# Routed experts of an audio tower: weights stationary and 512 rows moving in the upper products

## What is computed

```python
scores = jax.nn.softmax((xf @ gate_w).astype(jnp.float32), axis=-1)
_, sel = jax.lax.top_k(scores + expert_bias[None, :], TOPK)      # TOPK = 2, E = 8
...
token_idx = order // TOPK
routed_in = xf[token_idx] * top_scores_sorted[:, None]           # rows of one expert together
h = jax.nn.silu(jax.lax.ragged_dot(routed_in, w1, counts)) * jax.lax.ragged_dot(routed_in, w3, counts)
routed_out = jax.lax.ragged_dot(h, w2, counts)                   # w1, w3: 512 x 448, w2: 448 x 512
out = out.at[token_idx].add(routed_out)
```

## Time and profile before

| | us |
|---|---|
| median of 3 runs (6222.33 to 6225.37) | 6224.54 |
| the profiled execution | 6225.23 |
| its span, first to last instruction | 6223.5 |
| TensorE busy | 6034.7 |
| VectorE busy | 3931.3 |
| ScalarE busy | 2617.3 |
| GpSimd busy | 2608.1 |

### The profile page before, as it was taken

How to read it: one execution, slowest core, us unless ns; L and a number is a source line. 1 busy time by engine, 2 the same in 40 slices (tenths; PEclk the granted TensorE clock), 3 DMA queues, 4 the chain that set the end, 5 groups by cost and what they waited for, 6 DMA issues and landing times. The chain is left out here.

```text
span 6223.5 us, 108360 instructions
## 1 busy us (share of the span) xinstructions
PE 6034.7 (97%) x32968; PEld 5134.6 (83%) x32968; DVE 3931.3 (63%) x9812; ACT 2617.3 (42%) x4904; POOL 2608.1 (42%) x1865
## 2 busy tenths in 40 slices
PE   5999999999999999999999996999999999999999
PEld 4888888888888888888888885888888888888888
DVE  4777777777777777777777774444444444444444
ACT  3444444444444444444444442333333333333332
POOL 1333333333333333333333333555555655555554
PEclk8999999999999999999999998999999999999999
DMA  2111111111111111111111113555555555555541
GB/s 69 48 44 44 47 41 47 44 44 47 42 49 41 46 45 43 48 41 48 43 44 47 42 40 102 138 143 141 143 144 143 132 140 145 137 143 144 143 105 48
DMA packets 273407, 495.61 MB, mean 80 GB/s; under 512 B 39444, under 2 KB 112148, under 8 KB 273236
## 3 DMA queue, kind: packets, MB, share of 16 engines
q1 hardware_dynamic: 202452, 363.37, 19.6%
q0 software_dynamic: 70912, 131.71, 10.4%
HBM read 370.13 MB, written 140.28 MB: 82 GB/s over the span
## 5 line engine op out<-in xcount | busy, mean ns | idle before, releaser
L1325 POOL DMA_INDIRECT out_dram<-res,goal x280 | 519.4, 1855 | 929.9 <-DVE res L1261 446.1
L619 ACT ACTIVATE e<-ps,shift 128x512 f32<-128x512 f32 x512 | 347.9, 684 | 671.1 <-DVE shift L718 635.3
L1193 ACT ACTIVATE rT_hi<-ps 128x512 fp32r<-128x512 f32 x280 | 167.9, 600 | 1040.2 <-PE ps L1129 1040.2
L1119 PE MATMUL ps<-e_hi,rT_hi 128*128 128x448 f32 x2240 | 596.9, 388 | 5.2 <-ACT rT_hi L1193 5.2
L1303 POOL TENSOR_TENSOR e_lo<-raw,e_hi 128x1792 fp32r<-128x1792 f32 x140 | 568.6, 4062 | 9.8 <-ACT e_hi L1188 6.5
L1261 DVE COPY res<-ps 128x512 f32<-128x512 f32 x280 | 193.7, 692 | 594.8 <-PE ps L1119 579.8
L1119 PE MATMUL ps<-e_lo,rT_hi 128*128 128x448 f32 x2240 | 550.8, 367 | 0.0
L1119 PE MATMUL ps<-e_hi,rT_lo 128*128 128x448 f32 x2240 | 549.4, 367 | 0.0
L904 POOL TENSOR_SCALAR ve<-ag 125x1 f32<-125x1 f32 x256 | 57.1, 223 | 1124.7 <-DVE ag L734 1087.0
L1119 PEld LDWEIGHTS ps<-e_hi,rT_lo 128*128 128x128 f32 x2240 | 421.2, 188 | 37.8
L1119 PEld LDWEIGHTS ps<-e_lo,rT_hi 128*128 128x128 f32 x2240 | 421.2, 188 | 37.3
(11 more groups left out here) (203 smaller groups left out, 15377.0 us busy)
## 6 DMA issues: line engine op xcount, KB each, us to landing
raw<-in_L_ffn_w SPq DMA_DIRECT2D x210, 896.0 KB, 5.6
X<-in_x SPq DMA_DIRECT2D x128, 750.0 KB
normed_rows<-y SPq DMA_DIRECT2D x128, 250.0 KB
out_dram<-h SPq DMA_DIRECT2D x128, 250.0 KB
rows<-normed_rows,entries POOLq DMA_INDIRECT x280, 4.8
out_dram<-res,goal POOLq DMA_INDIRECT x280
routed_entries<-entry,slot POOLq DMA_INDIRECT x256
raw<-in_L_ffn_sw SPq DMA_DIRECT2D x3, 896.0 KB
```

Of the source, the lines that this page charges most:

```text
L619: nc.scalar.activation(e[:, i, :], ps[:, (i + 1) % 2, :], ACT.Exp, scale=QS, bias=shift[:, i:i + 1], accum_out=total[:, i:i + 1]).then_inc ...
L1119: ins = nc.tensor.matmul(dst, lhs[a][:rows_, k, :], rhs[b][:rows_, k, 0:width], start=(k == 0 and i == 0), stop=(k == KC - 1 and i == 2))
L1325: nc.gpsimd.indirect_dma_start(out, bass.IndirectOffsetOnAxis(ap=goal[group[1] % 2][:, i:i + 1], axis=0), res[i % 2][:], None, bounds_chec ...
```

## The change

The upper products swap their roles. Stationary is now a block of 128 columns of a weight, moving are all 512 turned rows of the group, so the inner values come out with their columns on partitions and the four transposes per tile of `turn_hidden` go. The 448 columns are three full chunks of 128 and a tail of 64. w1 and w3 lie side by side in one tile (`W13`), w3 with its tail first, so that one block of 128 columns holds the tails of both; `up` (12 matmuls) runs 7 times a group. The lower product takes the inner values as they are: 3 full chunks in three passes, 9 matmuls, and a tail of 2 matmuls over 128 partitions, which hold the high part above and the low part below, against w2's tail stored twice: 11 matmuls a tile instead of 12.

With that, rows are scaled by their score on ScalarE (`scale_rows`, in place) before they are turned, and `half`, `half2` go; the turned rows of the whole group must be complete before its first product; turned rows and inner values have one buffer for a group instead of two for a tile. The gate of the tail needs w3's half, which sits on the upper 64 partitions, so ScalarE copies it to `evb` first. `inner_lo` and the last product of the tail's gate read two SBUF tiles. There are four result buffers instead of two, and `down` alternates between two PSUM banks. GpSimd's order is new: add 2, gathers 0 and 1, add 3, gathers 2 and 3, both splits, adds 0 and 1. w3 is fetched with two DMAs and w2 with three.

The core of the diff:

```diff
-            raws = (raw1, raw3, raw2)
-            W = [tuple((sbuf(f"e{n}_hi{p}", r.shape, F32R, c2), sbuf(f"e{n}_lo{p}", r.shape, F32R, c2))
+            W13 = [[sbuf(f"up_{part}{p}", [P, KC, 2 * HID], F32R, c2) for part in ("hi", "lo")] for p in range(2)]
+            W2 = [[sbuf(f"down_{part}{p}", [P, T, D], F32R, c2) for part in ("hi", "lo")] for p in range(2)]
+            rT = [sbuf(f"rT_{part}", [P, KC, GROUP], F32R, c2) for part in ("hi", "lo")]
+            uT = [sbuf("uT_hi", [P, T, GROUP], F32R, c2), sbuf("uT_lo", [P, FULL, GROUP], F32R, c2)]
+            res = [sbuf(f"res{i}", [P, D], F32, c2) for i in range(T)]
...
+                        sp.dma_start(raws[1][:, :, 0:TAIL], third[:, :, FULL * P:HID]).then_inc(w_in[1].of(group), 16)
+                        sp.dma_start(raws[1][:, :, TAIL:HID], third[:, :, 0:FULL * P]).then_inc(w_in[1].of(group), 16)
...
+                    def up(group, bank, col):
+
+                        w = W13[group[1] % 2]
+                        for i, (a, b) in enumerate(PASSES):
+                            for k in range(KC):
+                                ins = nc.tensor.matmul(ps[:, bank, :], w[a][:, k, col:col + P], rT[b][:, k, :],
+                                                       start=(k == 0 and i == 0), stop=(k == KC - 1 and i == 2))
+                        return ins
...
+                        if i == 0:
                             pe.wait_ge(w_lo[2].sem, w_lo[2].at(group))
+                            pe.wait_ge(uT_lo.sem, uT_lo.at(tile_of(group, FULL - 1)))
+                        pe.wait_ge(res_sb.sem, res_sb.at(back(t, 2)))
+                        for n, (a, b) in enumerate(PASSES):
+                            for k in range(FULL):
+                                nc.tensor.matmul(ps[:, 6 + i % 2, :], uT[a][:, k, i * P:(i + 1) * P], w[b][:, k, :],
+                                                 start=(k == 0 and n == 0), stop=False)
+
+                    def down_tail(group, i):
+
+                        w = W2[group[1] % 2]
+                        if i == 0:
+                            pe.wait_ge(uT_lo.sem, uT_lo.at(tile_of(group, FULL)))
...
+                        pe.wait_ge(w_lo[0].sem, w_lo[0].at(group))
+                        pe.wait_ge(w_lo[1].sem, w_lo[1].at(group))
+                        pe.wait_ge(rT_lo.sem, rT_lo.at(tile_of(group, T - 1)))
+                        for c in range(FULL):
+                            pe.wait_ge(gb_sb.sem, gb_sb.at(back(tile_of(group, c), 2)))
+                            up(group, 2 + 2 * (c % 2), c * P).then_inc(u_ps.sem, 1)
+                            up(group, 3 + 2 * (c % 2), HALF + c * P).then_inc(u_ps.sem, 1)
+                        pe.wait_ge(gb_sb.sem, gb_sb.at(back(tile_of(group, FULL), 2)))
+                        up(group, 4, FULL * P).then_inc(u_ps.sem, 2)
+                        if not last:
+                            turn_rows(after, 0)
+                            turn_rows(after, 1)
+                        down_full(group, 0)
+                        down_full(group, 1)
+                        down_tail(group, 0)
+                        down_tail(group, 1)
+                        if not last:
+                            turn_rows(after, 2)
+                            turn_rows(after, 3)
+                        for i in (2, 3):
+                            down_full(group, i)
+                            down_tail(group, i)
...
+                        tanh(group, 0)
+                        if not last:
+                            split_up(after, 0)
+                        inner_hi(group, 0)
+                        if not last:
+                            split_up(after, 1)
+                        tanh(group, 1)
+                        inner_hi(group, 1)
+                        if not last:
+                            scale_rows(after, 0)
+                            scale_rows(after, 1)
+                        tanh(group, 2)
+                        inner_hi(group, 2)
+                        tanh(group, 3, TAIL)
+                        act.wait_ge(gb_sb.sem, gb_sb.at(back(tile_of(group, 3), T)))
+                        nc.scalar.activation(vb[0:TAIL, :], ps[TAIL:P, 4, :], ACT.Copy).then_inc(vb_sb.sem, 1)
...
+                    def inner_lo(group, c):
+                        t = tile_of(group, c)
                         dve.wait_ge(uT_hi.sem, uT_hi.at(t))
+                        if c < FULL:
+                            nc.vector.tensor_tensor(uT[1][:, c, :], gb[c % 2][:], uT[0][:, c, :].bitcast(F32),
+                                                    ALU.subtract).then_inc(uT_lo.sem, 1)
...
+                        gate(group, 0)
+                        inner_lo(group, 0)
+                        split_down(group)
+                        for c in (1, 2):
+                            gate(group, c)
+                            inner_lo(group, c)
+                        gate(group, 3)
+                        if not last:
+                            rows_lo(after, 0)
+                        inner_lo(group, 3)
...
+                            add_rows(before, 2)
+                        if not last:
+                            gather(after, 0)
+                            gather(after, 1)
+                        if not first:
+                            add_rows(before, 3)
+                        if not last:
+                            gather(after, 2)
+                            gather(after, 3)
+                            split_up(after, 0)
+                            split_up(after, 1)
+                        add_rows(group, 0)
+                        add_rows(group, 1)
```

More of the change, by code:

```diff
@@ L1027, in audio_tower @@
[L1027 to L1033, removed]
@@ L1050, in audio_tower @@
+            scaled, rT_hi, th_sb, vb_sb, uT_hi = (tiles("t_" + n) for n in ("scaled", "rT_hi", "th_sb", "vb_sb", "uT_hi"))
+            goal_sb = tiles("goal_sb")
             rT_lo, ga_sb, gb_sb, uT_lo, res_sb = (tiles("t_" + n) for n in ("rT_lo", "ga_sb", "gb_sb", "uT_lo", "res_sb"))
@@ new lines, in split_down, with scale_rows @@
+                    def split_down(group):
+                        act.wait_ge(w_in[2].of(group), w_in[2].at(group))
+                        act.wait_ge(d_ps.sem, d_ps.at(tile_of(back(group, 2), T - 1)))
+                        nc.scalar.activation(W2[group[1] % 2][0][:], raws[2][:], ACT.Copy).then_inc(w_hi[2].sem, 1)
+                    def scale_rows(group, i):
+                        act.wait_ge(rows_in[i], landed(group))
+                        nc.scalar.activation(rows[i][:], rows[i][:], ACT.Copy,
+                                             scale=entries[group[1] % 2][:, i, 1:2]).then_inc(scaled.sem, 1)
@@ L1252, in hidden_lo @@
[L1252 to L1258 removed]
+                    for i in range(T):
+                        nc.vector.memset(rows[i][:], 0.0).then_inc(cleared, 1)
@@ L1291, in work @@
-                        if last:
-                            hidden_lo(tile_of(group, T - 1))
-                            result(tile_of(group, T - 1), T - 1)
+                            goals(group)
+                            for i in range(T):
+                                rows_lo(group, i)
+                        gate(group, 0)
+                        inner_lo(group, 0)
+                        split_down(group)
+                        for c in (1, 2):
+                            gate(group, c)
+                            inner_lo(group, c)
@@ new lines, in work @@
+                        gate(group, 3)
+                        if not last:
+                            rows_lo(after, 0)
+                        inner_lo(group, 3)
+                        if not last:
+                            rows_lo(after, 1)
+                        result(group, 0)
+                        result(group, 1)
+                        if not last:
+                            rows_lo(after, 2)
+                            rows_lo(after, 3)
+                        result(group, 2)
@@ L1294, in _ @@
+                        result(group, 3)
+                        if not last:
+                            goals(after)
                     each_group(dve, work)
@@ L1322, in add_rows @@
                         pool.wait_ge(added.sem, added.at(back(t, 1)))
[L1323 removed]
+                        pool.wait_ge(goal_sb.sem, goal_sb.at(group))
                         alone(pool)
```

312 lines of the change are left out of this document (139 added, 173 removed).

## The result

The changed kernel takes 6496.48 us (median of 4 runs, 6487.82 to 6502.85), the kernel before 6223.43 (6221.76 to 6225.37): a ratio of 1.0438, interval 1.042 to 1.0456. It is slower by 4.4%, where 1.2% faster was forecast, and it lies above the range of 6005 to 6270. Its profiled execution has a span of 6492.4 us.

A forecast was written before the change was run, and what follows sets the result against it. TensorE's matmuls bound the group loop; 30.8 us of work plus 2.1 of stalls gave a 32.9 us period, and 3832.1 + 69 x 32.9 + 44.5 = 6147, stated as 6150 us, 1.2% faster, range 6005 to 6270.

The forecast's parts named there:

- Start and end: Outside the group spacings: first up product at 3832 us, 7.5 later; last group 44.5 us instead of 45.8.
- The matmuls: TensorE's work per group: 128 matmuls at 227.5 ns plus 16 transposes, 30.8 us, 3.3 less than before.
- the other end: Upper price of a matmul, 234 ns instead of 227.5, adding 0.8 us to a group.
- Cost 0; with rows 2 us later it would be 1.: ScalarE's scaling of gathered rows ahead of tanh of chunk 2: tanh starts at 14.5 instead of 13.9, no loss.
- The exclusion: VectorE passes with two SBUF inputs wait behind GpSimd's splits, stalling TensorE 2.1 us a group.
- until 19.4: VectorE's inner_lo 2, due at 17.9, waits for the first split's end only; TensorE stalls 0.2 us.
- GpSimd's steps: GpSimd's queue, add to add: 5.2 us a step, so the splits begin at 15.3 us of the group.
- The slower rival: GpSimd's serial queue decides: steps of 6 and more, splits from 17.7, stalls 3.5 to 4.5 us; chance 0.22.
- SP, w3 in two pieces, the split w2: Weight fetches in more DMAs and packets, and SP's longer list: cost 0, if the cover holds.

The follow-up runs named there:

- e4_both: Changed kernel with inner values left in PSUM until split, and rows 0 and 1 scaled after inner_hi of chunk 2: 6090.56 us, ratio 0.9793.
- e1_psum: Changed kernel with only the inner values left in PSUM until split, so no VectorE pass there has two SBUF inputs: 6291.32 us.
- e2_scale_late: Changed kernel with only ScalarE's order changed, rows 0 and 1 of the next group scaled after inner_hi of chunk 2: 6485.85 us.
- e10_splits_apart: e2_scale_late plus one wait: GpSimd issues its second split only once VectorE's inner_lo 2 is through; 6243.9 us.
- e7_gathers_first: e1_psum with GpSimd issuing gathers 0 and 1 of the next group ahead of add 2 instead of behind it: 6254.35 us.
- e8_rows112: e4_both with up's matmuls reading 112 of the 128 partitions of both operands: 6099.27 us.

## Why the prediction was wrong, step by step

The forecast's period was 32.9 us, the measured one 37.95. The difference of 5.05 is made up of 2.6 of gap (4.7 for 2.1), 1.8 of clock and 0.7 of pace; 69 x 5.05 = 348 us, against 6492.4 - 6146.7 = 346 between the spans (start and end came 3 us shorter than forecast).

- **Start and end.** Right. The first `up` came at 3831.22 (3832.1 forecast), and the last group took 42.5 (44.5).
- **The matmuls.** The count was right, the price a little off: 233 ns, near the other end (234), and so 128 x 0.0055 = 0.7 us a group more. The saving of 3.3 became 2.6. e4_both shows what it is worth without stalls: 31.93 us a group for 34.10.
- **"Cost 0; with rows 2 us later it would be 1."** This cover failed. The step took 4.8 us for the landing of a gather, from a kernel in which the gathers stood one to a tile. Here two are issued together, the first of them held by VectorE's split_down (2.25 us instead of 1.05, the very effect of rows 7, applied to the add and not to the gather), and the fetch of w2 is issued between them, 10.3 us into the group. Gather 0 landed 14.6 us into the group (forecast 12.5) and gather 1 at 19.0 (13.8), so `tanh` of chunk 2 started at 19.7. Alone this costs 2.7 us of gap a group (e1_psum), where the step had 0, and 1 for rows 2 us later.
- **The exclusion.** The mechanism was right and is shown twice: L1325 of up to 7.6 us where GpSimd reads SBUF, 0.69 always where the pass reads PSUM. The rule of the Trainium skill (SBUF — State Buffer, Who interferes with whom) agrees, in that the second of the two blocks. But the step let `inner_lo` 2 through at the end of the first split ("until 19.4"), where it waits to the end of the second. That makes 4.6 us of gap (e2_scale_late), not 0.2 + 1.9; with a turn between, it is 0.6 + 1.8 (e10_splits_apart). The same section's inference that descriptor writing isn't hit by a pass of two SBUF inputs is contradicted again, by the gathers of 2.25, 2.51 and 2.73 us.
- **The clock.** No term of the sum. A gap of 4.4 us was followed by 3.6 us at the lower level, 1.8 us a group; the gaps of 1.5 to 1.8 in e10_splits_apart, of the size that the forecast had, never were. In e1_psum, behind gaps of 2.5 to 2.8, the clock fell in 22 of 48 groups, and `down` took 11.05 on average, so 0.8 more. So this term is a consequence of the two steps above.
- **GpSimd's steps.** Nearly right: from add to add 5.5 to 5.6 us in the median (5.2 forecast), splits at 16.4 (15.3). The slower rival named the right side but another cause. It wanted steps of 6 and more; the splits began before its 17.7, and the loss came all the same.
- **SP, w3 in two pieces, the split w2.** Taken as 0. In e4_both ScalarE never waits for their loads. The gathers, which share the DMA engines with them, land 6.5 to 7.1 us after their issue in the median in most versions, but after 4.5 in e7_gathers_first and 4.6 in e8_rows112, which have the same extra DMAs; so the extra DMAs alone don't make them late. What differs is where a gather stands to w2's fetch (issued at 10.3 to 11.5 us of the group). In the changed kernel gathers 0 and 1 go at 8.5 and 10.8 us and land 6.4 and 8.5 later. In e8_rows112 they go behind it, at 13.8 and 15.2, and land 5.2 and 4.5 later; in e7_gathers_first gather 0 goes 3 us ahead of it and takes 4.5, gather 1 goes at 8.6 and takes 8.0. That points to the overlap with this fetch; no run changes it alone.

Two steps of the prediction thus failed, and each is enough for a gap before `down_full` 0. One is "Cost 0" for the rows in front of `tanh` of chunk 2: it took a landing time from another spacing of the same transfers, gather 1 came 5.2 us later than that, and this alone costs 2.7 us of gap. The other is "waits until 19.4", 0.2 us, for `inner_lo` 2: it waits for both splits, and this alone makes 4.6 us of gap. Where both are present the gap is 4.7, and the lower clock behind it, which was no term of the sum, adds 1.8. The change itself is sound: keeping the inner values in PSUM until they are split, and scaling the rows after the chunk that is waited for, make 6090.56 us, 2.1% less than the kernel before (1.9 to 2.3).

## What to carry to other kernels

When an edit moves a two-input pass of VectorE from PSUM to SBUF, ask which GpSimd instructions that read SBUF run beside it, and price the wait up to the end of all that stand back to back, not of one; a wait between them, or one input in PSUM, takes most of it away. Put a pass that waits for a DMA behind the passes of the same queue that TensorE waits for, and give a landing time from one spacing no margin in another. When two delays end at the same instruction, remove both before judging either: here one alone gave 0.2 us, the other 3.0, and both 6.0. When a stall is gone, look for the next limit just behind it: here it is GpSimd's queue.

## What the runs showed of the hardware

- A VectorE pass with two SBUF inputs waits through two GpSimd instructions that stand back to back (6.60 and 8.38 us for a pass of 0.69), also with 64 partitions (3.91 behind what was left of the pair), and is let in when GpSimd has to wait for it (2.69).
- Writing descriptors on GpSimd is held by VectorE's two-SBUF split: 2.25 to 2.73 us for a gather that takes 1.05.
- After a gap of 4.4 us the granted clock was 0.54 for 3.6 us (1.8 us lost), behind the gaps of 2.5 to 2.8 us in e1_psum it fell in 22 of 48 groups (0.8 us lost on average), behind those of 1.5 to 1.8 in e10_splits_apart it stayed at 1.00; filling the gap with 20 matmuls of no use made the kernel 81 us faster.
- The median landing of a 256 KB gather moved from 4.8 us to between 6.5 and 7.1 where gathers were issued beside the fetch of w2; where most of them were not, it was 4.5 and 4.6.
- With GpSimd's splits, gathers and adds in one queue, add 0 issued 0.2 us behind the splits was followed by the next add only 7.6 us later (e7_gathers_first), where the steps of the changed kernel had medians of 5.5 to 5.6.
